# Second attention: softmax weights scaled on GpSimd and turned with the plain identity, in a redrawn list of steps

## The reference

```python
h = _rms_norm(x, ada[:, None, :], EPS_NORM)
qkv = h @ qkv_w.T                       # q, k, v: 4 heads of 64
q, k = _scale_for_cosine_sim(q, k, scale[:, None, None], EPS_COS)
q, k = _rope(q, k)
scores = jnp.einsum('bhle,bhme->bhlm', q, k)
scores = jnp.where(mask, scores, NEG_INF)
attn = jax.nn.softmax(scores, axis=-1)
o = jnp.einsum('bhlm,bhme->bhle', attn, v)
o = jnp.transpose(o, (0, 2, 1, 3)).reshape(n, l, d)
return o @ out_w.T + skip
```

## Time and profile before

| | |
|---|---|
| median of three runs | 268.54 us (267.06 to 268.93) |
| span of the profiled execution | 266.0 us |
| PE busy | 232.5 us, 87% |
| DVE busy | 202.7 us, 76% |
| ACT busy | 154.9 us, 58% |
| POOL busy | 117.4 us, 44% |
| mean granted clock of PE, share of full speed | 0.987 |

### The profile page before, as it was taken

One profiled execution on the slowest core, in us unless ns is written; L12 is line 12 of the kernel. 1 busy time (PEld: TensorE's weight loads), 2 busy tenths in 40 slices (PEclk: granted clock), 3 DMA queues, 4 the chain that ended last, 5 costly groups with the idle time before them and its releaser, 6 DMA issues.

```text
span 266.0 us, 4823 instructions
## 1 busy us (share of the span) xinstructions
PE 232.5 (87%) x1710; PEld 186.4 (70%) x1710; DVE 202.7 (76%) x421; ACT 154.9 (58%) x303; POOL 117.4 (44%) x184
## 2 busy tenths in 40 slices
...
DMA packets 8248, 10.11 MB, mean 38 GB/s; under 512 B 1824, under 2 KB 7072, under 8 KB 8224
## 3 DMA queue, kind: packets, MB, share of 16 engines
...
## 4 chain that ended last, share of the span: by engine, by line
PE 51%; DVE 16%; ACT 11%; issue 8%; POOL 7%; DMA 3%; SPq 2%; ACTq 0%; DVEq 0%; POOLq 0%
PE ring L785 8%; PE ring L786 7%; PE ring L787 7%; PE ring L791 6%; PE ring L838 5%; PE psx L863 5%; PE pv L883 4%; DMA xs<-in_x 3%; PE ring L1047 3%; DVE nm L1153 3%; ACT kstk L673 3%; ACT kstk L672 2%; PE pv L1062 2%; ACT ps L598 2%; POOL nt L450 1%
## 5 line engine op out<-in xcount | busy, mean ns | idle before, releaser
L1153 DVE TENSOR_REDUCE nm<-ring 128x2 f32<-128x512 f32 x64 | 40.2, 683 | 5.3 <-PE ring L838 5.2
L598 ACT ACTIVATE ps<-psx 128x1024 f32<-128x1024 f32 x32 | 31.3, 1026 | 7.5 <-PE psx L863 4.3
L838 PE MATMUL ring<-kstk,qstk 128*128 128x512 f32 x64 | 25.0, 449 | 4.1 <-ACT kstk L673 2.7
L785 PE MATMUL ring<-wqkv_hi,xm_hi 128*128 128x512 f32 (+1 forms) x64 | 24.3, 379 | 4.4 <-DVE xm_lo L1146 2.9
L786 PE MATMUL ring<-wqkv_lo,xm_hi 128*128 128x512 f32 (+1 forms) x64 | 23.3, 364 | 0.0
L787 PE MATMUL ring<-wqkv_hi,xm_lo 128*128 128x512 f32 (+1 forms) x64 | 22.9, 358 | 0.0
L838 PEld LDWEIGHTS ring<-kstk,qstk 128*128 128x128 f32 x64 | 11.3, 193 | 13.9 <-DVE nm L1153 5.3
L791 PE MATMUL ring<-ident,stack 128*128 128x128 f32 x128 | 17.7, 278 | 2.9 <-ACT kstk L673 1.4
L863 PE MATMUL psx<-qstk,kstk 128*128 128x256 f32 x128 | 19.7, 287 | 0.3 <-ACT ps L598 0.3
L863 PEld LDWEIGHTS psx<-qstk,kstk 128*128 128x128 f32 x128 | 17.8, 189 | 2.5 <-ACT ps L598 0.9
L883 PE MATMUL pv<-ps,vs 128*32 128x256 f32 x256 | 16.1, 383 | 3.6 <-issue 3.3
...
## 6 DMA issues: line engine op xcount, KB each, us to landing
...
```

The source lines that it names most:

```text
L598: a.activation(ps[:, n % 4], psx[:, n % 2], ACT.Exp).then_inc(exp_done, 1)
L785: mm(dst, lhs[0], rhs[0], start=start, stop=False)
L838: last = mm(dst, qstk[:, b % 2, p, qc * P:(qc + 1) * P], kstk[:, b % 2, 2 * p:2 * p + 2, :], start=True, stop=not with_bias)
L1153: v.tensor_reduce(nm[:, qc, :, p], bank(key).rearrange("p (h n) -> p h n", h=2), AX.X, ALU.max, negate=True).then_inc(ring_dve, 1)
```

## The change

`diag` and its semaphore go. `diag1` on DVE only inverts the sums. A new step, `scale1` on POOL (L563 of the changed kernel), multiplies the weights of one tile (four heads, 128x1024) by the inverse sums, in place. For the last batch POOL scales two heads (128x512) and DVE the other two, in `diag1` (L1396). `turnp1` on PE waits for the scaled weights and turns them with the plain identity through the kernel's `transposes`, as `turn1` does. The list of steps is redrawn over the whole program; `scale1` stands in it eight times, which makes 415 entries. In the part before the MLP the moves are small swaps (for instance, `value0:2.0` now stands ahead of `score0:2.4`, `split_w1` behind `score0:2.7`, `zeros:1` behind `hi0:1.1`); in the second part `qk1:1.0` moves from ahead of `fc2:3` to behind it, and `square1`, `cos`, `rope` and `turnp1` steps change places with the new ones.

```diff
@@ ORDER, two of the 35 lines before and of the 36 after
...
-rope:2.0 cos:1.1 turnp1:0.1 exp1:1.0 rope:2.1 qk1:3.0 qk1:3.1 diag1:1.0 max1:1.1 value1:0 turn1:2.0 rsums1:3
-diag1:1.1 turn1:2.1 heads1_lo:0 exp1:1.1 root1:1 square1:2.0 square1:2.1 cos:2.0 heads1:0 turnp1:1.0 cos:2.1
...
+cos:2.0 root1:2 value1:0 heads1:0 rope:2.0 qk1:3.0 qk1:3.1 rope:2.1 cos:2.1 turn1:2.0 turn1:2.1 heads1_lo:0
+diag1:1.1 v1:3 scale1:1.0 square1:3.0 square1:3.1 scale1:1.1 score1:2.0 score1:2.1 rsums1:3 max1:2.0 max1:2.1
...
@@ -282,7 +283,7 @@
         weights_q = (ps[:, 2], ps[:, 3])
         weights_k = (ps[:, 0:2].rearrange("p s i k n -> p s (i k) n"),
                      stage_b[:, :].rearrange("p (k h n) -> p k h n", k=TB, h=H1))
-        diag = o_raw[:, :, :].rearrange("p s (h n) -> p s h n", h=H1)
+        weights_h = [w.rearrange("p i f n -> p (i f) n") for w in weights_q]
         v1 = vs[:, :, :, :, :].rearrange("p s t h d -> p s t (h d)")[:, :, :, 0:C]
 
         psx = ctx.enter_context(nc.psum_tensor("psx", [P, 2, 2, TB, L], F32))
@@ -319,7 +320,8 @@
         at_ready = sem("heads_ready")
         sq1_ready, seed1_ready, rn1_ready = sem("sq1_ready"), sem("seed1_ready"), sem("rn1_ready")
         cos_done, rope_done = sem("cos_done"), sem("rope_done")
-        max1_ready, diag_ready, heads1_hi = sem("max1_ready"), sem("diag_ready"), sem("heads1_hi")
+        max1_ready, heads1_hi = sem("max1_ready"), sem("heads1_hi")
+        inv1_ready, even_scaled, odd_scaled = sem("inv1_ready"), sem("weights_scaled_pool"), sem("odd_weights_scaled_vector")
         h_hi_ready, h_lo_ready = sem("h_hi_ready"), sem("h_lo_ready")
         s_out = sem("out_stored")
         dve_step, pool_step = sem("vector_step"), sem("pool_step")
@@ -553,6 +555,13 @@
                                     qk[:, t % TB, :].rearrange("p (g d) -> p g d", d=D1 // 2),
                                     rope_sb[:, t % TB, 0:1, :].to_broadcast([P, 4 * H1, D1 // 2]),
                                     ALU.mult).then_inc(cos_done, 1)
+                if name == "scale1":
+                    m = 2 * b + i_
+                    heads = 2 if b == B - 1 else H1
+                    pool.wait_ge(inv1_ready, m + 1)
+                    w = weights_h[m % 2][:, 0:heads, :]
+                    g.tensor_tensor(w, w, inv1[:, m % 2, 0:heads].unsqueeze(2).to_broadcast([P, heads, L]), ALU.mult)\
+                     .then_inc(even_scaled, 1)
                 if name == "head_scales":
 
                     pool.wait_ge(s_row, 16)
@@ -743,7 +752,7 @@
                     act.wait_ge(max1_ready, m + 1)
                     if m >= 2:
                         act.wait_ge(*full(("P1", (m - 2) // 2, m % 2, 1)))
-                        act.wait_ge(diag_ready, m - 1)
+                        act.wait_ge(inv1_ready, m - 1)
                     n = PAIRS * B + m
                     for i in range(2):
                         for f in range(FC):
@@ -1039,14 +1048,13 @@
                         last.then_inc(s_full, 1)
                     if name == "turnp1":
                         m = 2 * b + i_
-                        pe.wait_ge(exp_done, PAIRS * B + m + 1)
-                        pe.wait_ge(diag_ready, m + 1)
+                        pe.wait_ge(even_scaled, m + 1)
+                        if b == B - 1:
+                            pe.wait_ge(odd_scaled, i_ + 1)
                         for kc in range(TB):
                             dst = claim(("P1", b, i_, kc))
-                            for h in range(H1):
-                                last = mm(dst[:, h * P:(h + 1) * P], weights_q[m % 2][:, h % 2, h // 2, kc * P:(kc + 1) * P],
-                                          diag[:, m % 2, h, :], start=True, stop=True)
-                            last.then_inc(ring_full, 1)
+                            transposes(dst, [weights_q[m % 2][:, h % 2, h // 2, kc * P:(kc + 1) * P] for h in range(H1)])\
+                                .then_inc(ring_full, 1)
                     if name == "value1":
 
                         pe.wait_ge(*emptied(("v1", b)))
@@ -1379,15 +1387,14 @@
 
                     m = 2 * b + i_
                     dve.wait_ge(exp_done, PAIRS * B + m + 1)
-                    step(v.reciprocal(inv1[:, m % 2, :], sums1[:, m % 2, :]))
                     if m >= 2:
-                        dve.wait_ge(*full(("P1", (m - 2) // 2, m % 2, 1)))
-                    elif m == 0:
-                        dve.wait_ge(*full(("oT", B - 1, 1)))
-                    v.tensor_tensor(diag[:, m % 2].rearrange("p (f i) n -> p f i n", i=2),
-                                    ident[:, :].unsqueeze(1).unsqueeze(1).to_broadcast([P, FC, 2, P]),
-                                    inv1[:, m % 2, :].rearrange("p (i f) -> p f i", i=2).unsqueeze(3)
-                                    .to_broadcast([P, FC, 2, P]), ALU.mult).then_inc(diag_ready, 1)
+                        dve.wait_ge(even_scaled, m - 1)
+                    v.reciprocal(inv1[:, m % 2, :], sums1[:, m % 2, :]).then_inc(inv1_ready, 1)
+                    if b == B - 1:
+                        dve.wait_ge(inv1_ready, m + 1)
+                        w = weights_h[m % 2][:, 2:H1, :]
+                        v.tensor_tensor(w, w, inv1[:, m % 2, 2:H1].unsqueeze(2).to_broadcast([P, 2, L]), ALU.mult)\
+                         .then_inc(odd_scaled, 1)
                 if name == "turnp1":
                     key = ("P1", b, i_, 1)
                     dve.wait_ge(*full(key))
```

More of the change, by code:

```diff
@@ L76 @@
 ORDER = [(name, *map(int, filter(None, rest.split(".")))) for name, _, rest in (word.partition(":") for word in """
[L77 to L105, removed]
@@ L111 @@
-heads1_lo:2 heads1:2 turnp1:3.0 turnp1:3.1 root1:3 heads1_lo:3 proj1:2 value1:3 proj1:3 cos:3.1 heads1:3
+const_sel silu const_v stats0:0 norm0:0 ada split_wqkv0 normed0:0 head_scales zeros:0 const_stack split0:0
+qk0:0.0 stats0:1 qk0:0.1 square0:0.0 square0:0.1 stats0:2 norm0:1 root0:0 sums0:0 v0:0 norm0:2 normed0:1
+split0:1 ada_rest stats0:3 bias_count normed0:2 unit0:0.0 hi0:0.0 hi0:0.1 v0:1 unit0:0.1 square0:1.0 square0:1.1
+flag lo0:0.0 qk0:1.0 lo0:0.1 root0:1 qk0:1.1 norm0:3 turnk0:0.0 turnk0:0.1 sums0:1 gamma_rows turnq0:0.0
@@ new lines @@
+turnq0:0.1 split0:2 max0:0.0 normed0:3 max0:0.1 max0:0.2 unit0:1.0 unit0:1.1 qk0:2.0 qk0:2.1 lo0:1.0 v0:2
+hi0:1.0 hi0:1.1 zeros:1 gamma:0 max0:0.3 gamma:1 max0:0.4 lo0:1.1 turnk0:1.0 max0:0.5 max0:0.6 sums0:2
+turnk0:1.1 turnq0:1.0 max0:0.7 neg0:0 turnq0:1.1 gamma:2 shift0:0 max0:1.0 mask gamma:3 max0:1.1 max0:1.2
+score0:0.0 max0:1.3 square0:2.0 score0:0.1 score0:0.2 max0:1.4 square0:2.1 unit0:2.0 unit0:2.1 score0:0.3
+split0:3 max0:1.5 value0:0.0 split_wproj root0:2 value0:0.1 max0:1.6 xbias0:0 hi0:2.0 hi0:2.1 lo0:2.0 score0:0.4
@@ new lines @@
+qk0:3.0 square0:3.0 take0:0.0 max0:1.7 score0:0.5 score0:0.6 qk0:3.1 neg0:1 turnk0:2.0 score0:0.7 lo0:2.1
+square0:3.1 out0:0.0 value0:0.2 shift0:1 turnq0:2.0 turnq0:2.1 turnk0:2.1 value0:0.3 sums0:3 max0:2.0 take0:0.1
+score0:1.0 max0:2.1 score0:1.1 max0:2.2 score0:1.2 score0:1.3 max0:2.3 unit0:3.0 value0:1.0 unit0:3.1 hi0:3.0
+max0:2.4 score0:1.4 score0:1.5 take0:1.0 hi0:3.1 out0:0.1 max0:2.5 value0:1.1 lo0:3.0 max0:2.6 heads0:0
+score0:1.6 score0:1.7 root0:3 max0:2.7 neg0:2 value0:1.2 heads0_lo:0 shift0:2 lo0:3.1 turnk0:3.0 proj0:0
@@ new lines @@
+turnq0:3.0 turnq0:3.1 stats1:0 turnk0:3.1 value0:1.3 take0:1.1 max0:3.0 score0:2.0 max0:3.1 score0:2.1 out0:1.0
+score0:2.2 out0:1.1 norm1:0 score0:2.3 max0:3.2 value0:2.0 max0:3.3 heads0:1 score0:2.4 max0:3.4 score0:2.5
+heads0_lo:1 take0:2.0 max0:3.5 value0:2.1 max0:3.6 score0:2.6 score0:2.7 xbias1:0 xbias0:1 xbias1:1 max0:3.7
+neg0:3 proj0:1 normed1:0 shift0:3 split_w1 take0:2.1 stats1:1 value0:2.2 value0:2.3 score0:3.0 out0:2.0 out0:2.1
+score0:3.1 v0:3 score0:3.2 xbias0:2 score0:3.3 heads0:2 value0:3.0 value0:3.1 heads0_lo:2 xbias1:2 take0:3.0
@@ new lines @@
+score0:3.4 score0:3.5 proj0:2 score0:3.6 score0:3.7 stats1:2 norm1:1 split_w2 value0:3.2 take0:3.1 value0:3.3
+split1:0 out0:3.0 xbias0:3 normed1:1 out0:3.1 norm1:2 split1:1 heads0_lo:3 fc1:0.0 fc1:0.1 fc1:0.2 heads0:3
+fc1:0.3 gelu:0.0 gelu:0.1 gelu:0.2 gelu:0.3 fc1:1.0 fc1:1.1 fc1:1.2 xbias1:3 proj0:3 stats1:3 gelu:1.0 gelu:1.1
+gelu:1.2 normed1:2 split_wqkv1 split1:2 fc2:0 norm1:3 fc1:1.3 fc1:2.0 fc1:2.1 stats2:0 norm2:0 cos:0.0 cos:0.1
+normed1:3 gelu:1.3 fc1:2.2 fc1:2.3 split1:3 split2:0 gelu:2.0 gelu:2.1 normed2:0 square1:0.0 square1:0.1
```

13 lines of the change are left out of this document (10 added, 3 removed).

## The result

The changed kernel takes 280.74 us (median of 4 runs, 279.23 to 285.35); the kernel before, on the same chip, 268.74. The ratio is 1.045 (95% interval 1.038 to 1.053), so it is slower by some 12 us. Every ratio in this document compares the fast executions of a kernel with those of the kernel before on the same chip, so it isn't exactly the quotient of two medians. The prediction was 276.7 us, with a range of 262 to 282.

What follows compares the result with a forecast made beforehand. Second attention's legs were taken as bound by DVE and what holds it up, the tail by PE. 3.5 + 5.4 + 3.7 - 1.9 - 2.5 = +8.2 on a 266.0 span, plus 2.5 around it: 276.7 us, range 262 to 282.

Steps and rivals of the forecast that it cites:

- part before the legs: Part before the MLP: less waiting by ACT for `value0:2.0`, guessed between 0 and -5 us, taken as -2.5.
- leg 1: Second attention, from PE's end of `fc2:3` to DVE's last multiplication of `rope:1.1`: 17.5 us against 14.0, +3.5.
- leg 2: Second attention, from there to DVE's last multiplication of `rope:2.1`: 19.4 us against 14.0, +5.4.
- leg 3: Second attention, from there to DVE's last multiplication of `rope:3.1`: 17.8 us against 14.1, +3.7.
- tail: After the last `rope:3.1` multiplication: four cheaper turns save 3.8 us on PE, last batch's scaling adds about 2; -1.9.
- the exclusion: A POOL product and a two-operand DVE operation in SBUF take turns; DVE work reading PSUM isn't affected.
- Rope rows beside `scale1`: Sign in the legs: DVE rope rows beside `scale1` stretched to 1.5 to 2.9 us; at 0.69, the exclusion is wrong.
- the turn of eight: Sign on PE: eight transposes of weights with the identity take 1.06 us, against 2.02 with the diagonal.
- all the added work hides: Rival: `scale1` falls beside DVE's PSUM work or doesn't exclude DVE; second attention about -4.1, 262 us; chance 0.2.
- the dear turn: Rival: eight transposes take the diagonal's 2.02 us, the tail loses its 3.8 gain; 280.5 us; chance 0.13 with "worse".
- Half hidden: Rival: two or three of the legs' five scalings run beside PSUM work, 271 us; chance 0.17.
- the lower bound of 2.08: Price of a 128x1024 `scale1` on POOL: at least twice a lone square, 2 x 1.04 us; 2.3 was taken.

## Why the prediction came out as it did

Side by side, in us of span against the kernel before:

| term | predicted | measured |
|---|---|---|
| part before the legs | -2.5 | +5.2, or +6.2 with the 1.0 below set back |
| leg 1, with `fc2:3` ending earlier | +3.5 | +3.7, less 1.0 |
| leg 2 | +5.4 | +3.5 |
| leg 3 | +3.7 | +1.7 |
| tail | -1.9 | -2.8 |
| sum | +8.2 | +11.3 |

(The 1.0: `v1:0`, the last PE work ahead of the moved step, ended 6.2 us late, `fc2:3` 5.2.)

**The direction, and the exclusion, were right.** Rope rows beside `scale1` were stretched to 2.00 and 2.11 us, within the 1.5 to 2.9 forecast; the turn of eight is at 1.0 us, and the tail is nearly 3 us shorter. The three legs came to 17.7, 17.5 and 15.8 us; 17 to 19 each had been named, and the third is below. The rival that all the added work hides falls, and so does the dear turn. Half hidden came true in part: two of the five scalings in the legs ran beside DVE's reductions. That the exclusion isn't the only price, the old list with the scaling shows: there the rope pair is bare, and the legs grow by 5.4 us through POOL's lateness, a wait that the prediction had named only as what is queued behind `scale1`.

**The sum was near by luck.** The step that failed is "the part before the MLP": "between 0 and -5, I take -2.5". It was a gain read off one wait of ACT, without pricing what took its place, and it came out as a loss of 5 to 6 us, which the front of the list shows by itself (ratio 1.024). Which steps of the front cost it stays open but for one late DMA. That loss and the overstated legs partly cancelled.

**The legs were overstated by 4.7** (12.6 against 7.9). The scaling was priced at 2.3 us, half of a subtraction of twice the size; a scaling without contention took 1.89, below even the lower bound of 2.08, and the mean of the six was 2.04. Five of them gave 11.5 in the sum; the run without their time gives 7.0. The prediction hadn't separated the rest of the replayed growth. The replayed legs were 14.1 longer; less 11.5 of scalings and with 3.5 of diagonals put back, 6.1 are left for the list, which is near the 5.2 that the new list with diagonals shows. The prediction then named the scaling as the cause of what was, to a good half, the list.

**"Four turns save 3.8, the scaling costs 2" in the tail** measured -2.8, of which the new list alone gives 0.2 (24.6).
